# The small blocks' third layer: from plain products to split ones, with its weights through the ring of stages

## The reference

```python
h = gelu(x @ w1[n] + b1[n])      # 512 -> 1024
h = gelu(h @ w2[n] + b2[n])      # 1024 -> 1024
y = h @ w3[n] + b3[n]            # 1024 -> 512
```

## Time and profile before

| what | us |
|---|---|
| median of three runs (1726.62 to 1728.06) | 1727.58 |
| the profiled execution | 1727.94 |
| its span | 1726.1 |
| TensorE busy, share of the span | 99% |
| DVE, ACT busy | 70%, 54% |
| the transfer engines, five slices from 993 us on | 80 to 98% |
| small blocks, about | 1011 to 1218 us |

### The profile page before, as it was taken

How to read it: one execution, slowest core, us unless ns; L and a number is a source line. 1 busy time by engine, 2 the same in 40 slices (tenths; PEclk the granted TensorE clock), 3 DMA queues, 4 the chain that set the end, 5 groups by cost and what they waited for, 6 DMA issues and landing times.

```text
span 1726.1 us, 40334 instructions
## 1 busy us (share of the span) xinstructions
PE 1707.1 (99%) x15462; PEld 1510.9 (88%) x15462; DVE 1209.7 (70%) x2807; ACT 931.6 (54%) x1652; POOL 180.2 (10%) x271
## 2 busy tenths in 40 slices
PE   9999999999999999999999999999999999999997
PEld 8878988898889888988898877787999999999997
DVE  5567777777777777777775466566677777777773
ACT  5655655565556555655555454455545555545551
POOL 2011110111011101110110100000001001111000
PEclk9999999999999999999999999999999999999999
DMA  9972222222222222221215499998666666667761
GB/s 302 390 286 78 83 88 72 72 83 88 60 84 83 88 64 80 82 89 46 79 39 176 154 369 383 350 354 291 197 218 214 208 203 205 213 224 225 218 198 47
DMA packets 128181, 292.72 MB, mean 170 GB/s; under 512 B 19610, under 2 KB 42842, under 8 KB 128040
## 3 DMA queue, kind: packets, MB, share of 16 engines
q1 hardware_dynamic: 104616, 225.46, 38.7%
q0 software_dynamic: 23424, 65.30, 12.6%
HBM read 244.04 MB, written 46.66 MB: 168 GB/s over the span
## 4 chain that ended last, share of the span: by engine, by line
PE 92%; DVE 2%; DMA 2%; ACT 1%; issue 1%; SPq 1%; POOLq 0%; POOL 0%; DVEq 0%; ACTq 0%
PE bank_rows L2288 21%; PE bank_rows L745 14%; PE bank_rows L731 13%; PE bank_rows L798 7%; PE bank_rows L2303 7%; PE bank_rows L2342 5%; PE bank_rows L786 4%; PE bank_rows L809 4%; PE bank_rows L2328 3%; PE bank_rows L2369 3%; PE bank_rows L825 3%; PE bank_rows L768 2%; PE bank_rows L889 1%; DVE probs L1460 1%; ACT probs L1138 1%
## 5 line engine op out<-in xcount | busy, mean ns | idle before, releaser
L1138 ACT ACTIVATE probs<-probs,neg_max 100x726 f32<-100x726 f32 x256 | 228.9, 896 | 174.4 <-DVE neg_max L1460 174.4
L1460 DVE CUSTOM_DVE_ANT_0 probs<-bank_rows,mask_sb 100x726 f32<-100x726 f32 x256 | 222.9, 909 | 22.0 <-PE bank_rows L786 14.6
L2532 DVE TENSOR_TENSOR w_low<-stage,w_high 128x1024 fp32r<-128x1024 f32 x176 | 213.3, 1222 | 34.2 <-ACT w_high L2436 33.3
L2436 ACT ACTIVATE w_high<-stage 128x1024 fp32r<-128x1024 f32 x176 | 183.7, 1057 | 32.0 <-DMA stage<-in_L_ffn_w 31.9
L2459 ACT ACTIVATE gelu<-bank_rows,biases 128x256 f32<-128x256 f32 x176 | 82.3, 474 | 217.4 <-PE bank_rows L2288 211.9
L1144 ACT ACTIVATE p_t<-bank_rows 122x1200 f32<-122x1200 f32 x128 | 146.5, 1168 | 97.1 <-PE bank_rows L798 97.1
L2288 PE MATMUL bank_rows<-h_high,w_low 128*128 128x256 f32 x704 | 196.6, 279 | 0.0
L2288 PE MATMUL bank_rows<-h_low,w_high 128*128 128x256 f32 x704 | 196.6, 279 | 0.0
L2288 PE MATMUL bank_rows<-h_high,w_high 128*128 128x256 f32 x704 | 196.6, 279 | 0.0
L731 PE MATMUL bank_rows<-ctx_high,wk_high 128*128 128x360 f32 (+1 forms) x512 | 175.7, 343 | 1.0 <-DVE v_even L1441 0.9
L731 PE MATMUL bank_rows<-ctx_low,wk_high 128*128 128x360 f32 (+1 forms) x512 | 167.9, 328 | 0.0
(11 more groups left out here) (245 smaller groups left out, 3851.0 us busy)
## 6 DMA issues: line engine op xcount, KB each, us to landing
stage<-in_L_ffn_w SPq DMA_DIRECT2D x240, 512.0 KB, 4.7
plain_w<-in_L_ffn_w SPq DMA_DIRECT2D x15, 2048.0 KB, 12.3
expert_in_rows<-filling POOLq DMA_DIRECT2D x8, 3341.0 KB, 23.6
router_rows<-in_gate_rows POOLq DMA_DIRECT2D x112, 200.0 KB, 3.3
ctx_raw<-in_ctx SPq DMA_DIRECT2D x16, 720.0 KB, 4.7
ctx_raw<-in_ctx SPq DMA_DIRECT2D x15, 724.0 KB, 4.4
xs_sb<-expert_in_rows SPq DMA_DIRECT2D x11, 514.0 KB, 5.3
b_sb<-in_L_ffn_b SPq DMA_DIRECT2D x19, 256.0 KB, 5.0
```

What stands on the lines that cost most here:

```text
L1138: nc.scalar.activation(p, p, ACT.Exp, bias=neg_max[:, h:h + 1], scale=-1.0, accum_out=exp_sum[:, h:h + 1]).then_inc(probs_ready, 1)
L1460: nc.vector.tensor_tensor_reduce(out=pieces(probs[:, q, :]), in0=slots_of(q)[0:S, :, 0:PIECE], in1=pieces(mask_sb[:]), scale=-1.0, scalar= ...
L2436: nc.scalar.activation(hi, src, ACT.Copy).then_inc(chunk_hi[which], 1)
L2532: nc.vector.tensor_tensor(lo, src, hi.bitcast(F32), ALU.subtract).then_inc(chunk_lo[which], 1)
```

## The change

w3 of a small block comes as four chunks of 512 KB (two row tiles of 128x512 each) through the same four places, behind the eight chunks of w2, and each is cast by ACT (`third_high`) and subtracted by DVE (`third_low`) into one pair of buffers. `second_gelu` runs twice for each tile, once into a float32r high part and once into a whole one, and DVE subtracts them in halves (`second_split`). The third layer becomes 24 split products. The order changes with it: third_high(j) and third_low(j) come first in the loop bodies of ACT and DVE; SP loads the rows and w1 of j + 2 ahead of all eight chunks of w2 of j + 1, and the chunks of w3 last. The first four w2 chunks now wait for third_low of the block before.

```diff
@@ -1955,12 +1956,14 @@
-    plain = {i: [placed(f"plain_w{i + 1}_{a}", [P, *shapes[i]], F32, at[2 * i + a]) for a in range(2)] for i in (0, 2)}
+    plain = [placed(f"plain_w1_{a}", [P, *shapes[0]], F32, at[a]) for a in range(2)]
     h_hl = [[placed(f"h{i + 1}_{n}", [P, HT, BLOCK], F32R, h_at + H_SHIFT + (2 * i + a) * HT * BLOCK * 4)
...
     small_h1 = [placed(f"small_h1_{n}", [P, HT, P], F32R, h_at + a * HT * P * 4) for a, n in enumerate(("high", "low"))]
-    small_h2 = placed("small_h2", [P, HT, P], F32, h_at + 2 * HT * P * 4)
+    small_h2_at = (h_at + 2 * HT * P * 4, start + SMALL_H_END + HT * BLOCK * 4)
+    small_h2 = [placed(f"small_h2_{n}", [P, HT, P], F32R, small_h2_at[a]) for a, n in enumerate(("high", "low"))]
+    small_h2_whole = placed("small_h2_whole", [P, HT, P], F32, small_h2_at[1])
     small_sums = placed("small_sums", [P, 2, D], F32, start + SMALL_H_END + 2 * HT * BLOCK * 4)
@@ -1981,8 +1984,10 @@
-    BASE = (0, HT * NSMALL, 0)
-    LOADS_BASE = HT * NSMALL // STAGES
+    BASE = (0, HT * NSMALL, HT // 2 * NSMALL)
+    SMALL_CHUNKS = HT + HT // 2
+    LOADS_BASE = SMALL_CHUNKS * NSMALL // STAGES
+    assert SMALL_CHUNKS % STAGES == 0 and HT // 2 == STAGES
@@ -2019,7 +2024,7 @@
             else:
-                sp.wait_ge(chunk_lo[1], BASE[1] - STAGES + i + 1)
+                sp.wait_ge(chunk_lo[2], BASE[2] - STAGES + i + 1)
             rows, _, kt = chunk_source(which, k)
@@ -2086,9 +2091,9 @@
-        def load_plain(j, e, which):
-            src = as_rows((w1, w2, w3)[which][bass.ds(e, 1), :, :]).rearrange("(t p) n -> p t n", p=P)
-            sp.dma_start(plain[which][j % 2][:], src).then_inc(plain_loaded[which][j % 2], 16)
+        def load_plain(j, e):
+            src = as_rows(w1[bass.ds(e, 1), :, :]).rearrange("(t p) n -> p t n", p=P)
+            sp.dma_start(plain[j % 2][:], src).then_inc(plain_loaded[j % 2], 16)
@@ -2099,15 +2104,26 @@
             src = as_rows(w1[bass.ds(e, 1), :, cols]).rearrange("(t p) n -> p t n", p=P)
-            sp.dma_start(plain[0][0][:, :, cols], src).then_inc(first_loaded[half], 16)
+            sp.dma_start(plain[0][:, :, cols], src).then_inc(first_loaded[half], 16)
...
             for k in ks:
-                if HT * j + k >= STAGES:
+                if k >= STAGES:
                     sp.wait_ge(chunk_lo[1], HT * j + k - STAGES + 1)
+                elif j > 0:
+                    sp.wait_ge(chunk_lo[2], HT // 2 * (j - 1) + k + 1)
                 sp.dma_start(stage[:, k % STAGES, :], as_rows(w2[bass.ds(e, 1), k * P:(k + 1) * P, :])
                              ).then_inc(chunk_loaded[k % STAGES], 16)
+        def load_third(j, e):
+            for i in range(HT // 2):
+                sp.wait_ge(chunk_lo[1], HT * j + HT - STAGES + i + 1)
+                rows = slice(2 * i * P, 2 * (i + 1) * P)
+                sp.dma_start(stage[:, i, :].rearrange("p (t n) -> p t n", t=2),
+                             as_rows(w3[bass.ds(e, 1), rows, :]).rearrange("(t p) n -> p t n", p=P)
+                             ).then_inc(chunk_loaded[i], 16)
@@ -2124,29 +2140,21 @@
         sp.wait_ge(early.first, HT // 2)
-        load_plain(1, e_next, 0)
+        load_plain(1, e_next)
         load_small_b3(0, e_now)
+        load_third(0, e_now)
         for j in range(NSMALL - 1):
...
                 e_after = small_expert(j + 2)
-            if 0 < j < NSMALL - 2:
-                load_small_rows(j + 2)
-            load_second(j + 1, e_next, FIRST_CHUNKS)
-            if j == 0:
-                load_plain(0, e_now, 2)
-                load_small_rows(2)
-            if j + 2 < NSMALL:
+                if j < NSMALL - 2:
+                    load_small_rows(j + 2)
                 sp.wait_ge(small_first, HT * (j + 1))
-                load_plain(j + 2, e_after, 0)
-            load_second(j + 1, e_next, LAST_CHUNKS)
-            if j == 0:
-                sp.wait_ge(early.y_ready, TPB)
-            else:
-                sp.wait_ge(y_ready, j)
-            load_plain(j + 1, e_next, 2)
+                load_plain(j + 2, e_after)
+            load_second(j + 1, e_next, range(HT))
             load_small_b3(j + 1, e_next)
...
                 load_small_biases(j + 2, e_after)
+            load_third(j + 1, e_next)
             e_next = e_after
@@ -2297,7 +2305,7 @@
                     if t == 0:
-                        pe.wait_ge(chunk_lo[2], CHUNKS_OF[2] * n + k // 2 + 1)
+                        pe.wait_ge(chunk_lo[2], BASE[2] + CHUNKS_OF[2] * n + k // 2 + 1)
                         pe.wait_ge(h2_lo, HT * n + k + 1)
@@ -2321,11 +2329,11 @@
                 elif j > 0 and m == 0:
-                    pe.wait_ge(plain_loaded[0][j % 2], 16 * (j // 2) + (0 if j % 2 == 0 else 16))
+                    pe.wait_ge(plain_loaded[j % 2], 16 * (j // 2) + (0 if j % 2 == 0 else 16))
                 if HT * j + m >= 2:
...
                 for k in range(DT):
-                    last = nc.tensor.matmul(first_bank[m % 2][:, 0:P], plain[0][j % 2][:, k, m * P:(m + 1) * P],
+                    last = nc.tensor.matmul(first_bank[m % 2][:, 0:P], plain[j % 2][:, k, m * P:(m + 1) * P],
                                             small_x[:, j % 2, k, :], start=(k == 0), stop=(k == DT - 1))
@@ -2363,11 +2371,13 @@
             for k in range(HT):
-                if k == 0:
-                    pe.wait_ge(plain_loaded[2][j % 2], 16 * (j // 2) + 16)
-                pe.wait_ge(small_second_gelu, HT * j + k + 1)
-                last = nc.tensor.matmul(small_y_bank(j)[:], small_h2[:, k, :], plain[2][j % 2][:, k, :],
-                                        start=(k == 0), stop=(k == HT - 1))
+                if k % 2 == 0:
+                    pe.wait_ge(chunk_lo[2], HT // 2 * j + k // 2 + 1)
+                if k % (HT // 2) == 0:
+                    pe.wait_ge(small_h2_lo, 2 * j + 2 * k // HT + 1)
+                for s, (a, c) in enumerate(PRODUCTS):
+                    last = nc.tensor.matmul(small_y_bank(j)[:], small_h2[a][:, k, :], w_hl[2][c][:, k, :],
+                                            start=(k == 0 and s == 0), stop=(k == HT - 1 and s == 2))
             last.then_inc(y_ready, 1)
@@ -2487,15 +2497,25 @@
             act.wait_ge(small_turned, 2 * j + half + 1)
-            nc.scalar.activation(small_h2[:, m, :], turned_bank[half][:, i * P:(i + 1) * P], ACT.Gelu,
+            src = turned_bank[half][:, i * P:(i + 1) * P]
+            nc.scalar.activation(small_h2[0][:, m, :], src, ACT.Gelu, bias=bias_of(j, 1, m))
+            nc.scalar.activation(small_h2_whole[:, m, :], src, ACT.Gelu,
                                  bias=bias_of(j, 1, m)).then_inc(small_second_gelu, 1)
...
                     act.wait_ge(small_w2_used, HT * (j - 1) + k + 1)
-                act.wait_ge(chunk_loaded[k % STAGES], 16 * ((HT * j + k) // STAGES + 1))
+                act.wait_ge(chunk_loaded[k % STAGES], 16 * ((SMALL_CHUNKS * j + k) // STAGES + 1))
                 nc.scalar.activation(w_hl[1][0][:, k, :], stage[:, k % STAGES, :], ACT.Copy).then_inc(chunk_hi[1], 1)
+        def third_high(j):
+            for i in range(HT // 2):
+                if j > 0 and i == 0:
+                    act.wait_ge(y_ready, j)
+                act.wait_ge(chunk_loaded[i], 16 * ((SMALL_CHUNKS * j + HT + i) // STAGES + 1))
+                nc.scalar.activation(w_hl[2][0][:, 2 * i:2 * i + 2, :], stage[:, i, :].rearrange("p (t n) -> p t n", t=2),
+                                     ACT.Copy).then_inc(chunk_hi[2], 1)
@@ -2506,11 +2526,13 @@
         for j in range(NSMALL - 1):
+            third_high(j)
             second_high(j + 1, FIRST_CHUNKS)
...
             second_high(j + 1, LAST_CHUNKS)
+        third_high(NSMALL - 1)
         for i in range(DT):
@@ -2620,6 +2642,19 @@
+        def third_low(j):
+            for i in range(HT // 2):
+                dve.wait_ge(chunk_hi[2], HT // 2 * j + i + 1)
+                at = slice(2 * i, 2 * i + 2)
+                nc.vector.tensor_tensor(w_hl[2][1][:, at, :], stage[:, i, :].rearrange("p (t n) -> p t n", t=2),
+                                        w_hl[2][0][:, at, :].bitcast(F32), ALU.subtract).then_inc(chunk_lo[2], 1)
+        def second_split(j, half):
+            at = slice(half * HT // 2, (half + 1) * HT // 2)
+            dve.wait_ge(small_second_gelu, HT * j + HT // 2 * (half + 1))
+            nc.vector.tensor_tensor(small_h2[1][:, at, :], small_h2_whole[:, at, :], small_h2[0][:, at, :].bitcast(F32),
+                                    ALU.subtract).then_inc(small_h2_lo, 1)
         def sums(j, half):
@@ -2645,6 +2680,7 @@
         for j in range(NSMALL - 1):
+            third_low(j)
             sums(j, 0)
@@ -2652,10 +2688,13 @@
                 split_first(j + 1, m)
+                if m % (HT // 2) == HT // 2 - 1:
+                    second_split(j, 2 * m // HT)
             if j + 2 < NSMALL:
...
             small_result(j)
+        third_low(NSMALL - 1)
         for i in range(3):
@@ -2664,6 +2703,8 @@
```

(5 more changed lines are left out.)

## The result

| | before | after |
|---|---|---|
| median, runs of both kernels on one chip | 1727.10 (1726.56 to 1728.06) | 1786.74 (1784.93 to 1787.86) |
| span of the profiled execution | 1726.1 | 1784.9 |
| ratio, 95% interval | | 1.0337 [1.0323, 1.0351] |

The kernel became slower by 59.6 us. The forecast was 1772, with 1744 to 1788 as its range: the direction and the mechanism held, the time stands at the upper end, 15 us above the sum.

The account below looks back on a forecast made before the run. TensorE was taken to bound the kernel before, with the transfer queue nearly full. Period terms 5 + 36.5 - 0.6 + 2.8 gave +43.7 us on 1727.94, forecast 1772 us, range 1744 to 1788.

Parts of the forecast that it names:

- The reading of before: Small blocks: TensorE end to end, 26.26 us a block, sets the end; transfers at a share of 1.00.
- Step 1: Small blocks' third layer on TensorE: 24 split products replace 16 plain passes, gaining 1.41 us a block, 11.3 over eight.
- Step 2: Work per block: ACT 19.8 us, DVE 22.7, both under 24.85, so neither is the bound by its sum alone.
- Step 3: Ring of four places, turning three times a period, with w1 ahead of w2's chunks: 33.6 us against 26.26, +7.3 a period.
- G: The moment ACT ends its last gelu of a block, from which the loop's times are counted; 1110.44 us in the earlier trace.
- Step 4: Where the longer loop applies: 5 + 36.5 - 0.6 + 2.8 = +43.7 us over the small blocks and tail.
- first period: First small-block period: w3 chunks issued early, landing 1013.9; first gelu 1028 against 1024.4, with DVE and clock +5 us.
- J = 6: Small-block period carrying no w1: 25.7 us, -0.6.
- tail: Big block's first w1 chunks wait for third_low(7), sums(7,1) comes about 4.5 later, last third layer 1.4 shorter: +2.8 us.
- A: Rival: all of it hidden, TensorE stays the bound at 24.85 us a block, 1716.6 us in all; chance 0.06.
- B: Rival: chunks overtake w1 in the transfers, periods of 25 to 26 us, 1724 to 1731 in all; chance 0.07.
- C: Rival: DVE's order makes TensorE wait for small_sums at its transposes, 27.3 to 29 us a period, 1735 to 1750; chance 0.09.

Follow-up runs that it names:

- the first profile: The changed kernel's first profiled execution, against the kernel before: median 1786.74 us against 1727.10, ratio 1.0337; mean period 35.2 us.
- the second: The changed kernel unaltered, run and profiled once more: 1786.89 us against 1727.81 for the kernel before, ratio 1.0335; mean period 34.4 us.
- the ten periods above: Five periods each of two variants of the changed kernel: w1 behind the first four w2 chunks (1755.55 us); no w1 loads for blocks 2 to 7 (1750.92).

## Why the prediction was right, and where it fell short

**The reading of before** held: nothing outside the small blocks moved by more than 1 us, and within them the bound went from TensorE to a chain through the ring.

**Step 1, the products:** right, 11.3 forecast and 11.4 measured with the products alone. **Step 2, the sums of ACT and DVE:** right, 19.1 and 22.4 a period against 19.8 and 22.7. That neither is the bound is shown by the version with w3 outside the ring, which does all this work in 24.8.

**Step 3, the loop:** the mechanism is shown, the size was too small, by 1.6 us a period in the first profile and by 0.8 in the second. Its points, after G, for the period from G at about 1109.25:

| | forecast | measured |
|---|---|---|
| issue of third(0) | 2.9 | 2.5 |
| third(0) down | 6.4 | 6.3 |
| third(3) down | 10.4 | 11.5 |
| w1 down | 17.3 | 19.6 |
| second(3) down | 23.7 | 24.7 |
| first gelu | 24.8 | 25.8 |
| next G | 33.6 | 35.1 |

Two terms were sized too small. From third(0) to third(3) it took 5.2 where three times 1.35 stood. The casts shown above say where: the steps between them are 2.53, 1.36 and 1.31, so the pace of 1.35 held for two of the three, and the first took nearly twice as long. By the landings, third(0) took 3.7 us, where I had 3.5, and the other three 5.1 to 5.5. And w1 with the rows ahead of it came 8.1 behind third(3) where 6.9 stood. The last four chunks then made up 1.3 (5.1 where 6.4 stood), being issued in time. From the first gelu to the next G it took 9.3 instead of 8.8.

The issue of third(0) had a flaw of the other sign. I put the half-tile subtraction in front with all of its 0.68, but the first subtraction of chunk 4 began only 0.3 later, 1.26 after G instead of 0.97. ACT now has one activation more behind the last gelu of the first layer, so DVE's last split of the hidden rows starts 0.21 before G, where it started 0.03 after it; and in the earlier trace rows the subtraction had waited about 0.1 for the cast.

**Step 4, the places where it applies.** Taking G as the issue of the biases just behind it:

| | forecast | measured |
|---|---|---|
| first period | +5 | +7.8 |
| five periods with w1 | +36.5 | +44.9 |
| J = 6, without w1 | -0.6 | +1.3 |
| tail | +2.8 | +5.6 |

These sum to 43.7 and 59.6; the small blocks began 0.4 earlier after the change, which leaves the span's 58.8 to within half a us. The chain of waits in the first period has its third(3) landing 7.62 after its issue, where I had taken 3.5. It stood in a queue: the w1 of block 1, issued at 998.6, was down at 1010.2, and the four chunks of w3 behind it landed one after another from 1012.4 to 1017.6. The chunk in that place before the change, issued at 1010.4, had taken 7.8 too, so the trace that I read the 3.5 from had the better number. J = 6 is dearer by its two landings, 5.12 and 4.70, where 3.9 and 3.5 stood.

In the tail the chain runs through the ring as well:

```profile
1247.34 6.04 DMA stage<-in_L_ffn_w
...
1255.88 5.63 DMA stage<-in_L_ffn_w
...
1267.92 0.61 DVE small_sums L2660
1268.58 0.66 PE bank_rows L2364 x4
```

The copy sums(7,1) began 25.1 after G (1242.7), where it had been 18.1 before the change: 7.1 later, where I had 4.5, and that is the error. (4.5 less 1.4 makes 3.1 besides, not 2.8.) A second wait of TensorE stands out there and costs nothing:

```profile
PE bank_rows L2271 <- DMA xs_sb<-expert_in_rows: 5.1, 1, 5.1
```

The big block's rows are loaded behind third(7), and TensorE stood for them, but it was done with the second layer 1.6 before the sums even so, and the wait isn't in the chain.

**The landings were sized too short throughout.** I took 3.5 from the shortest of a line's whole distribution, where the median was 6.2, and it fits only the first of four. A loop waits for the last of four loads, not for the luckiest single one; in the ten periods above it took 4.4 to 7.2. The bounds per period, 31.6 to 35.6, did hold the means of the two profiles, 34.4 and 35.2, though not the two single periods of 36.0 and 36.3, whose clock loss was larger than the full one that I had allowed: about 2.1 where the bound was 1.8. That the total fell inside the range is in part luck: it came 15 us above the sum, where the range left 16, and 5 of these 16 had been added for the landings without a row that gave their size.

**The rivals.** A (all hidden) fell: TensorE stood 8.03 us in the period shown, and 48.2 us in seven waits in all. Its time, 1716.6, is nearly reached by the version with w3 outside the ring, so the argument against it, that the loop forbids it, was the right one. B (chunks overtake w1) fell by the landings of 10.7 to 12.1 us. The Trainium skill, DMA: Bandwidth & Descriptors, "Queues, rings and completion order", says that completion is not in order for one issuing engine; it promises no order, and in the period shown the loads of 512 KB nevertheless did not come ahead of the 2048 KB one. B's price was wrong as well: with no w1 in the way, a period takes 27.3 to 31.0 and the kernel 1751, not 1724 to 1731 (25.1 to 26.0 over seven periods and 2.8 at the tail make 1723 to 1729 by themselves). C (DVE late at the transposes) did not happen: between 1000 and 1290 us TensorE waited for small_sums once, 1.6 us, against 48.2 us in seven waits for the gelu.

What the loss consists of, then, against the 1718.0 us measured with the cheaper products and nothing else: 33 us to the 1750.9 of a ring of twelve chunks with no w1 at all; 5 more for w1 behind the first chunks; 31 to 32 more for w1 ahead of them. The clock's 6.6 is in these.

## What to carry to other kernels

Buffers in a ring are a latency loop: count how often each place turns in a period, and multiply by a whole turn (issue, the last landing of the batch, cast, subtraction). Take the landing of the same load in the same place of the old trace, or the median, and not the shortest. Here a third turn cost some 30 us although every engine, and the transfer engines, had time to spare. On one queue, put a large load behind the small ones that somebody waits for soon: nothing but its place was worth 31 us.

When a step is put ahead of an instruction, ask first what that instruction was waiting for, and what else has moved on the engine: 0.69 us here made it only 0.3 later. And a long wait isn't a cost by itself: the tail's 5.1 us for the rows were followed by another wait that would have ended no sooner.

## What the runs showed of the hardware that I had not expected

- Loads queued behind a large one on the same queue landed after it: 10.7 to 12.1 us for 512 KB behind 2048 KB, against 3.7 to 5.5 for the four issued ahead of it in the same period.
- A share of 1.00 is not the end of what the transfer engines move. The earlier trace rows shows 354 GB/s at 1.00, but the kernel of before moved 393 at a share of 1.04 in its period from 1031.2 us on, and over its five busy slices the share was 0.87 to 1.03 (80 to 98% stands in the table of the time before). With w3 outside the ring it was 373 GB/s for 124 us, and TensorE never waited, although the eight chunks of 512 KB each took a median of 8.7 us to land.
- The last of four loads of 512 KB, issued within 4 us with nothing large about, landed after 4.4 us in one period and 7.2 in another of the kernel without w1. The cause is open.
- With stops of TensorE of some 8 us the granted clock of a period was 0.90, in two of ten 0.86, and the first two tiles behind one took 3.78 us instead of 1.95. With the stops filled by matmuls of no use it was 1.00 in all ten, and the timed runs were about 1 us shorter for each stop.
